# Attention stage of a transformer chain: side work of two engines dealt out between fills, the rows of maxima issued from ScalarE's queue, the second group's load held back

## The reference

```python
B, T, C, H = (2, 512, 256, 16); HD = C // H
qkv = (x @ w_qkv).reshape(Bx, Tx, 3, H, HD)
scores = jnp.einsum('bhqd,bhkd->bhqk', q, k) * SCALE
scores = jnp.where(causal[None, None], scores, -jnp.inf)
q_proj = jnp.einsum('bhtd,hd->bht', q[..., :8], head_dirs)
k_proj = jnp.einsum('bhtd,hd->bht', k[..., :8], head_dirs)
scores = scores + head_scales[None, :, None, None] * (q_proj[..., :, None] * k_proj[..., None, :])
attn = jax.nn.softmax(scores, axis=-1)
out = jnp.einsum('bhqk,bhkd->bhqd', attn, v)
# around it: h = layernorm(x) * (1 + ca) + sa;  x = x + ga * (out @ w_out)
```

## Time and profile before

| | us |
|---|---|
| median of 3 runs | 2779.84 |
| the profiled execution: time, span | 2780.32, 2778.2 |
| before the attention's first scores | 1254 |
| first scores to the start of the expert stages, about | 1007 |
| the expert stages | 517 |

### The profile page before, as it was taken

How to read it: one execution, slowest core, us unless ns; L and a number is a source line. 1 busy time by engine, 2 the same in 40 slices (tenths; PEclk the granted TensorE clock), 3 DMA queues, 4 the chain that set the end, 5 groups by cost and what they waited for, 6 DMA issues and landing times. The chain is left out here.

```text
span 2778.2 us, 45597 instructions
## 1 busy us (share of the span) xinstructions
PE 2366.8 (85%) x15266; PEld 1791.3 (64%) x15266; DVE 1525.3 (55%) x3440; ACT 1282.9 (46%) x2197; POOL 518.5 (19%) x429
## 2 busy tenths in 40 slices
PE   7999999999869999647888888888888877159997
PEld 6777777777658888525555555555555557149996
DVE  4544444444345454355666666666666646766664
ACT  2444444444445554624555555555555545024442
POOL 0111111111111111510110000100011013026663
PEclk8999999999989999768999999999999988569998
DMA  3200000000010000122333223223232207435542
GB/s 112 88 0 0 0 0 0 0 0 0 0 31 0 0 0 0 38 69 68 73 75 80 73 74 79 74 70 80 69 77 71 70 24 263 118 111 127 126 89 34
DMA packets 121392, 157.18 MB, mean 57 GB/s; under 512 B 24800, under 2 KB 102000, under 8 KB 121200
## 3 DMA queue, kind: packets, MB, share of 16 engines
q1 hardware_dynamic: 106992, 130.90, 17.2%
q0 software_dynamic: 14336, 25.44, 4.7%
HBM read 96.78 MB, written 58.98 MB: 56 GB/s over the span
## 5 line engine op out<-in xcount | busy, mean ns | idle before, releaser
L1461 DVE TENSOR_REDUCE at_top<-psum 128x1 f32<-128x512 f32 (+3 forms) x1024 | 447.2, 485 | 300.3 <-PE psum L1237 299.7
L1588 ACT ACTIVATE at_probs<-psum 128x512 f32<-128x512 f32 (+1 forms) x768 | 365.8, 530 | 346.5 <-PE psum L1255 344.5
L1235 PE MATMUL psum<-at_k_stack,at_q_stack 96*128 96x512 bf16 (+3 forms) x1024 | 295.4, 315 | 128.0 <-DMA at_k_stack<-qk_parts 72.5
L1253 PE MATMUL psum<-at_q_stack,at_k_stack 98*128 98x512 bf16 (+3 forms) x1024 | 288.9, 309 | 23.1 <-ACT at_probs L1588 16.8
L1235 PEld LDWEIGHTS psum<-at_k_stack,at_q_stack 96*128 96x128 bf16 x1024 | 103.1, 101 | 229.2 <-DVE at_top L1461 102.3
L1237 PE MATMUL psum<-at_mask_q,at_ident_b 128*128 128x128 bf16 x1024 | 206.3, 227 | 0.0
L1255 PE MATMUL psum<-at_mask_k,at_ident_b 128*128 128x128 bf16 x1024 | 202.4, 224 | 0.0
L1253 PEld LDWEIGHTS psum<-at_q_stack,at_k_stack 98*128 98x128 bf16 x1024 | 102.5, 100 | 115.1 <-issue 44.2
L1271 PE MATMUL psum<-at_probs,at_values 128*32 128x512 f32 (+3 forms) x2048 | 151.1, 436 | 0.9 <-ACT at_probs L1588 0.9
L570 POOL TENSOR_TENSOR y<-y,mean 128x512 f32<-128x512 f32 x64 | 83.2, 1333 | 364.8 <-ACT mean L623 364.8
L2312 POOL DMA_INDIRECT out<-ex_result,slot_tokens x64 | 119.6, 1869 | 102.8 <-DVE ex_result L2444 88.2
(11 more groups left out here) (404 smaller groups left out, 6142.1 us busy)
## 6 DMA issues: line engine op xcount, KB each, us to landing
qk_parts<-at_q_parts SPq DMA_DIRECT2D x96, 128.0 KB
qk_parts<-at_k_parts SPq DMA_DIRECT2D x96, 128.0 KB
at_q_stack<-qk_parts SPq DMA_DIRECT2D x64, 192.0 KB
at_k_stack<-qk_parts SPq DMA_DIRECT2D x64, 192.0 KB
x_residual<-in_x SPq DMA_DIRECT2D x16, 512.0 KB, 8.4
at_q_stack<-qk_parts SPq DMA_DIRECT2D x64, 128.0 KB
at_k_stack<-qk_parts SPq DMA_DIRECT2D x64, 128.0 KB
token_rows<-ro_h_tok SPq DMA_DIRECT2D x16, 512.0 KB, 3.0
```

Of the source, the lines that this page charges most:

```text
L1235: pe.matmul(out, q_stack[0:STACK, h, qt * P:(qt + 1) * P], k_stack[0:STACK, h, 0:w], start=True, stop=True)
L1253: pe.matmul(bank(bk)[:, col:col + w], k_stack[0:STACK + N_SHIFT, h, kt * P:(kt + 1) * P], q_stack[0:STACK + N_SHIFT, h, kt * P:T], start=T ...
L1461: dve.tensor_reduce(top[:, h, qt:qt + 1], bank(MAX0 + n % 2)[:, col:col + w], AX.X, ALU.max).then_inc(mxr.sem, 1)
L1588: act.activation(probs[:, slot(h), 512 * f:512 * f + w], bank(f)[:, 0:w], ACT.Exp).then_inc(ex.sem, 1)
```

## The change

- VectorE and ScalarE: the loops over heads get an inner loop over fills, and side work stands between single fills. Some pieces move to the next head (`dve_normal` from heads 4, 7, 10, 13 to the first fill of 5, 8, 11, 14; the second `dve_add` from 11 to 13; `act_values` from 3 to 4; `act_delta` from 8, 9 to 9, 10; the query and key conversions from heads 0, 1 to heads 1, 2, 3). TensorE's second `pe_turn_delta` moves from head 11 to 12, and `pe_turn_max` from behind the third fill to behind the second.
- The rows of maxima are issued by ScalarE (`act_row`) behind the exponential of the third fill of heads 2, 6, 10 and 14, no longer by SyncE.
- SyncE keeps stores and loads, in order; the load of group 1 now also waits for the landing of group 2's rows of the batch before.

```diff
 def act_batch(act, i, first, last, turn):
     for h in range(HEADS):
-        act_exp(act, i, h, first)
-        if h % GROUP == 0 and not (first and h == 0):
...
-        if h in (0, 1) and not last:
-            for n in range(2):
-                act_qk(act, i + 1, 2 * h + n)
-            for n in range(2):
-                act_qk2(act, i + 1, 2 * h + n)
-        if h == 3 and not last:
-            act_values(act, i + 1)
-        if h == 6 and not first:
-            act_o_hi(act, i - 1)
-        if h in (8, 9) and not first:
-            act_delta(act, i - 1, h - 8)
-        if h == 14 and turn:
-            act_hT(act, i + 2)
+        for f in range(3):
+            act_exp(act, i, h, f, first)
+            if f == 2 and h % GROUP == 0 and not (first and h == 0):
+                act_keep_oT(act, *((i, h // GROUP - 1) if h else (i - 1, NG - 1)))
+            if h == 1 and not last:
+                if f < 2:
+                    act_qk(act, i + 1, f)
+                else:
+                    act_qk2(act, i + 1, 0)
+            if h == 2 and f < 2 and not last:
+                if f == 0:
+                    act_qk2(act, i + 1, 1)
+                act_qk(act, i + 1, 2 + f)
+            if f == 2 and h % GROUP == 2 and not (last and h + GROUP > HEADS):
+                g = h // GROUP
+                act_row(act, *((i, g + 1) if g + 1 < NG else (i + 1, 0)))
+            if h == 3 and f < 2 and not last:
+                act_qk2(act, i + 1, 2 + f)
+            if h == 4 and f < 2 and not last:
+                act_values(act, i + 1, (f,))
+            if h == 6 and f < 2 and not first:
+                act_o_hi(act, i - 1, (f,))
+            if h in (9, 10) and f == 0 and not first:
+                act_delta(act, i - 1, h - 9)
...
 def dve_batch(dve, i, first, last, norm):
...
+                if h == 1 and f < 2 and not last:
+                    dve_qk_rest(dve, i + 1, f)
+                if h == 2 and f > 0 and not last:
+                    dve_qk_rest(dve, i + 1, 1 + f)
...
+                if h == 12 and f > 0 and norm:
+                    dve_norm(dve, i + 2, False, (2 * f - 2, 2 * f - 1))
...
+def act_row(act, b, g):
+    act.wait_ge(*neg(b, N_SHIFT * (g + 1)))
+    for j in range(N_SHIFT):
+        act.dma_start(q_stack[STACK + j:STACK + j + 1, ...], neg_top[:, j, :]).then_inc(row[g].sem, 16)
...
 def sp_load(sp, b, g):
     if not (isinstance(b, int) and b == 0):
         sp.wait_ge(*stp(b - 1, 3 * GROUP * (g + 1)))
     if g == 0:
         sp.wait_ge(*stored(b, stored.per))
+    elif g == 1 and not (isinstance(b, int) and b == 0):
+        sp.wait_ge(*row[2](b - 1, row[2].per))
...
-def sp_batch(sp, i, last):
-    sp_row(sp, i, 1)
-    if not last:
-        sp_store(sp, i + 1, 0)
-        sp_store(sp, i + 1, 1)
-    sp_row(sp, i, 2)
-    if not last:
-        sp_load(sp, i + 1, 0)
-        sp_load(sp, i + 1, 1)
-    sp_row(sp, i, 3)
-    if not last:
-        sp_load(sp, i + 1, 2)
-        sp_row(sp, i + 1, 0)
-        sp_load(sp, i + 1, 3)
+def sp_batch(sp, i):
+    for side in range(2):
+        sp_store(sp, i + 1, side)
+    for g in range(NG):
+        sp_load(sp, i + 1, g)
```

More of the change, by code:

```diff
@@ L1343, in pe_batch @@
                         pe_max(pe, i + 1, h + AHEAD - HEADS, f)
[L1344 to L1351, removed]
+                    if f == 1 and h % GROUP == 1 and not (last and h + GROUP > HEADS):
+                        g = h // GROUP
+                        if g:
+                            pe.wait_ge(*oe(i, g))
+                        else:
+                            pe.wait_ge(*(neg(i, N_SHIFT) if first else oe(i - 1, NG)))
+                        pe_turn_max(pe, *((i, g + 1) if g + 1 < NG else (i + 1, 0)))
                 if h in (0, 1) and not last:
@@ L1382, in pe_batch @@
                         pe_turn_delta(pe, i - 1, 0)
-                if h == 11 and not first:
+                if h == 12 and not first:
                     pe.wait_ge(*xs(i - 1, 1))
@@ L1432, in _, with dve_stats, dve_moments @@
                 pe_turn_delta(pe, b, n)
-        def dve_stats(dve, b):
-            for n in range(TT):
+        def dve_stats(dve, b, tiles=range(TT)):
+            for n in tiles:
                 tile = x[:, bass.ds(b * TT + n, 1), :].rearrange("p a d -> p (a d)")
                 dve.bn_stats(stats[:, n, :], tile).then_inc(s_stat.sem, 1)
+        def dve_moments(dve, b):
             for n in range(TT):
@@ L1444, in dve_stats, with dve_norm @@
             dve.tensor_scalar(var_eps[:, :], moments[:, :, 1], EPS, None, ALU.add).then_inc(s_eps.sem, 1)
-        def dve_norm(dve, b, first=False):
-            if not first:
+        def dve_norm(dve, b, first=False, tiles=range(TT)):
+            if not first and tiles[0] == 0:
                 dve.wait_ge(*lnt(b - 1, DK))
             dve.wait_ge(*s_pow(b, 1))
-            for n in range(TT):
+            for n in tiles:
                 tile = x[:, bass.ds(b * TT + n, 1), :].rearrange("p a d -> p (a d)")
@@ L1501, in dve_qk_rest, with dve_o_lo @@
                               ALU.subtract).then_inc(qr.sem, 1)
-        def dve_o_lo(dve, b):
-            for f in range(DK):
+        def dve_o_lo(dve, b, fs=range(DK)):
+            for f in fs:
                 dve.wait_ge(*yh(b, f + 1))
@@ L1515, in dve_batch @@
             for h in range(HEADS):
[L1516 to L1526, removed]
@@ L1554, in _ @@
             dve_stats(dve, 1)
+            dve_moments(dve, 1)
             dve_norm(dve, 1)
@@ L1641, in act_batch @@
             for h in range(HEADS):
-                act_exp(act, i, h, first)
-                if h % GROUP == 0 and not (first and h == 0):
-                    act_keep_oT(act, *((i, h // GROUP - 1) if h else (i - 1, NG - 1)))
-                if h in (0, 1) and not last:
-                    for n in range(2):
-                        act_qk(act, i + 1, 2 * h + n)
-                    for n in range(2):
-                        act_qk2(act, i + 1, 2 * h + n)
-                if h == 3 and not last:
-                    act_values(act, i + 1)
@@ L1659, in _ @@
         @block.scalar
         def _(act):
-            act_hT(act, 0)
+            for k in range(DK):
+                act_hT(act, 0, k)
+            for k in range(DK):
+                act_hT_hi(act, 0, k)
             for m in range(2):
@@ L1667, in _ @@
             act_values(act, 0)
-            act_hT(act, 1)
+            for k in range(DK):
+                act_hT(act, 1, k)
+            for k in range(DK):
+                act_hT_hi(act, 1, k)
+            act_row(act, 0, 0)
             act_batch(act, 0, True, False, True)
```

128 lines of the change are left out of this document (74 added, 54 removed).

## The result

| | us |
|---|---|
| kernel before, median of 5 runs beside it | 2782.65 (2778.41 to 2786.03) |
| changed kernel, median of 5 runs | 2799.8 (2795.63 to 2801.88) |
| ratio | 1.0061, 95% interval 1.0046 to 1.0076 |
| predicted | 2708, range 2670 to 2758 |

The change makes the kernel slower by 0.6%, 17 us. The forecast was faster by 72, so it missed by 89 us and in sign, and the time lies outside the range.

The account below looks back on a forecast made before the run. TensorE was taken to bound the stage, so only waits and what hangs on them could be won: 4.9 us a batch by 14 = 69, plus 3 for the first batch, 2780.3 - 72 = 2708 us, range 2670 to 2758.

Parts of the forecast that it names:

- First load: Head 9: load issued earlier without rows ahead of it, TensorE's wait falls from 3.4 to 0.6, saving 2.8 us a batch.
- Rows on ScalarE: Eight row issues a batch on ScalarE, median landing 1.7, tightest at head 8: loss of 0.6 us a batch, bounds 0 and 5.
- The third row as a rival: Group 2's rows wait behind the first load in flight, landing 3.8, TensorE waits 2.0 at head 8: 2730 us, chance 0.25.
- The prediction's sentence on the Trainium skill: SyncE's and ScalarE's DMAs share 16 engines, so the new queue doesn't speed a row meeting the first load; upper landing 3.79.
- Clock: Behind head 9's load wait: the low clock costing 1.6 us a batch mostly goes, winning 1.4, bounds 0 and 1.6.
- Side work: Pieces dealt out between fills cut TensorE's waits on VectorE and ScalarE by 1.3 of 4.5 us a batch.
- Sum a batch: All terms over one attention batch: 2.8 + 1.4 + 1.3 - 0.6 = 4.9 us saved, by 14 = 69.
- The slower rival: Rows on ScalarE cost SyncE's slowest issues and landing, waits at heads 8, 12, 0 and 4: 2839 us, chance 0.08.

Follow-up runs that it names:

- e7_row_early: Changed kernel with the rows issued by ScalarE behind the first fill of heads 2, 6, 10, 14 instead of the third: 2796.93 us, ratio 1.0047.
- e8: Changed kernel with group 2's rows back on SyncE before the first load, and nine single-copy DMAs a load instead of six: 2690.87 us, ratio 0.9667.
- e5: Kernel before, with each broadcast copy of a load issued as its own DMA, nine a load instead of six: 2693.39 us, ratio 0.9676.
- e1: Changed kernel's side work, but SyncE's queue as in the kernel before, with the rows on it ahead of the loads: 2795.6 us, ratio 1.0036.
- e2_queue: Kernel before with its side work in one piece, but rows on ScalarE and SyncE's queue as in the changed kernel: 2803.74 us, ratio 1.0081.
- e6_no_hold: Changed kernel without the second load's new wait for group 2's rows: 2810.97 us, ratio 1.0101.
- e4_split_after: Changed kernel with each broadcast copy of a load issued as its own DMA, nine a load instead of six: 2697.39 us, ratio 0.9694.
- e3_row2_on_sync: Changed kernel with only group 2's rows issued by SyncE again, between the stores and the first load: 2794.43 us, ratio 1.0036.

## Why the prediction was wrong

- **First load**, 2.8 forecast: the load wait went altogether, 3.4 a batch. Key stores 3.4 later and load 1.6 earlier, as worked out. Right, and a little more. (The start of head 2's exponentials, given as 1582.3, comes out as 1582.95 by the subtraction that is said to give it; nothing else hangs on the 0.7.) What the sum left out is that the load, 1.6 us earlier and beside a later row, is now in flight at the row's issue.
- **Rows on ScalarE**, a loss of 0.6 forecast: this is the step that failed. It took the median landing of 1.7, with 3.79 as the upper end, for a row that would now be issued with a whole load in flight. In the trace before no row had met more than a load's tail. Those of groups 1 and 2 met none and took 1.7 in all middle batches. Those of groups 3 and 0, issued 3.0 and 1.6 us before a load's last signal in the batch of the earlier trace rows, took 1.7 to 3.1, a hint that was passed over; and 3.79 is the first row of the stage. The rows of group 2 now landed 6.3 us after the second issue, 6.85 after the first, and TensorE waited 3.8 a batch. The issue cost was right. The bound of 5 a batch was wide enough in sum, but it was meant for four rows that cost a little each; one row cost it all.
- **The third row as a rival** (0.25, 2730) had the place and the cause. Its price was capped at 3.79 to landing. With 6.8 and the clock it is the result. The prediction's sentence on the Trainium skill pointed at it; its price was to be had from the first load's 9.3 to 11.1 us: issued at 27 it ends at 37 or so, and a row behind it lands not much sooner than its tail.
- **Clock**, 1.4 won: lost instead. The low clock came with the new wait, 3.45 to 4.2 us, as it had with the old one of 2.83 and more. Over thirteen whole batches, after and after with the split differ by 5.9 a batch (64.9 and 59.0), of which 3.3 is the row wait (3.8 less 0.4). The rest, 2.6, I put down to the clock: 1.0 more than the 1.6 before. As a check, the clock is low for 95.2 us of fourteen batches instead of 64.6; half of the difference is 1.1 a batch, an estimate as if TensorE were busy throughout. The premise that waits up to 2.79 leave the clock alone was one case: in `e7_row_early` waits of 2.5 had low clock with them in every batch.
- **Side work**, 1.3 forecast: 0.2 (e8 against e5), and a loss of 12 us where the load wait is kept (e1), since it makes group 2's maxima 0.75 to 1 us later. The forecast counted waits on VectorE and ScalarE, and they fell by 1.3 a batch as forecast: from 62.9 to 44.5 in fourteen batches (28.7 for maxima, 15.8 new ones for side work). Whether by the parts it named was not tested. It took TensorE's busy time as fixed, which rose by 0.6 a batch, and did not ask at which end of the batch the waits fell.
- **Sum a batch**, in the runs: -3.4 load wait, +3.8 row wait, +1.0 clock, -0.2 side work: +1.2, by 14 = 17 us, which is the measured difference. The clock's term is a remainder, so this agreement is no proof of it. The slower rival (2839) worked with waits at four heads; there is one.

## What to carry to other kernels

A small DMA issued behind a large one is priced by the tail of the large one, not by its own usual landing: before you move an issue, draw the intervals of all transfers in flight at its new place. When a wait disappears because a load starts earlier, look at what that load now covers. And if a load's tail runs at one or two tenths of the DMA engines, look at its outermost dimension first: here three more DMA issues won 3.1% to 3.3%, and reordering around the slow load won nothing. Last, add up the waits before you explain a loss by them: they were fewer in the changed kernel and in `e2_queue`, both slower, and the loss stood in the busy time.

## What the runs showed of the hardware

- A DMA of 4 KB from ScalarE's queue landed in 1.7 us alone. Two of them behind an unsplit load on SyncE's queue were in 5.5 (`e2_queue`) to 8.4 us (`e6_no_hold`) after the first issue, behind a split one 3.9 (`e4_split_after`); two alone 2.3 (group 2 in `e3_row2_on_sync`, from SyncE).
- A DMA issue on ScalarE took 0.51 to 1.02 us (median 0.605), mostly under an ACTIVATE still running; two in a row before side work left it idle for 1.12 us.
- Loads with a broadcast of 3 and 2 copies outermost: 10.4 us for 768 KB; as single copies: 6.8 us.
- TensorE's clock did not go by the length of one wait alone. In the kernel before, single waits up to 1.1 us left it at 1.00. In the changed kernel it was 0.50 for 6.8 us with every row wait at head 8, 3.45 us and more, and so it was in `e7_row_early` with waits of 2.5 to 3.2. In `e2_queue` it was 0.50 with a wait of 2.0 to 2.1 and one of 0.6 to 1.4 behind it, and with one of 1.9 to 2.3 at head 0 in seven of fourteen batches. One wait of 2.79 before and one of 3.53 in `e3_row2_on_sync` had no low clock with them. The low clock began before the wait was over: 0.3 to 1.9 us before its end in the changed kernel, 1.6 to 2.5 in `e7_row_early`.
